# The last 14 units of two channel norms move from a tail into the row sweep behind them

## The reference: what is computed

```
x = x + conv0(_ln_c(x))              # norm 0, then four sweeps
t = tokens(x); t = t + ffn0(_ln_t(t))   # norm 1, mixture of experts
x = x + conv1(_ln_c(x))              # norm 2, then four sweeps
t = tokens(x); t = t + ffn1(_ln_t(t))   # norm 3, then a recurrence over 3600 tokens
```

## Time and profile before

| | |
|---|---|
| median of three runs | 4286.7 us (4286.59 to 4288.07) |
| profiled execution, its own time | 4284.66 us |
| its span (first to last instruction) | 4282.9 us |
| TensorE busy | 4142.7 us, 97% |
| VectorE busy | 1331.6 us, 31% |
| ScalarE busy | 2059.6 us, 48% |
| mean granted TensorE clock | 0.987 of full speed |
| loads of norm 0 into the ring | 144 with those of norm 1's source, 200 KB each, 3.7 us to landing |

### The profile page before, as it was taken

How to read it: one execution, slowest core, us unless ns; L and a number is a source line. 1 busy time by engine, 2 the same in 40 slices (tenths; PEclk the granted TensorE clock), 3 DMA queues, 4 the chain that set the end, 5 groups by cost and what they waited for, 6 DMA issues and landing times.

```text
span 4282.9 us, 138615 instructions
## 1 busy us (share of the span) xinstructions
PE 4142.7 (97%) x57258; PEld 3149.5 (74%) x57258; DVE 1331.6 (31%) x2528; ACT 2059.6 (48%) x8972; POOL 119.8 (3%) x243
## 2 busy tenths in 40 slices
PE   8999999998889999999998899999999999999999
PEld 2899999994452899999994366666666666666666
DVE  4555533334556655533335600000000000000000
ACT  5002344445545002334444366666666666666666
POOL 1000000000010000000000000000000000000000
PEclk9999999999999999999999899999999999999999
DMA  5000000003348000000006300000000000000000
GB/s 145 11 0 0 0 0 0 0 0 115 94 116 253 23 0 0 0 0 0 0 0 170 100 15 21 22 15 22 21 15 22 18 19 21 15 21 22 15 21 18
DMA packets 178458, 144.78 MB, mean 34 GB/s; under 512 B 110910, under 2 KB 177502, under 8 KB 178014
## 3 DMA queue, kind: packets, MB, share of 16 engines
q1 hardware_dynamic: 177486, 137.58, 12.2%
q10 hardware_dynamic: 528, 0.63, 0.1%
HBM read 79.19 MB, written 58.98 MB: 32 GB/s over the span
## 4 chain that ended last, share of the span: by engine, by line
PE 94%; DVE 3%; issue 1%; ACT 1%; DMA 0%; SPq 0%; POOL 0%; DVEq 0%; ACTq 0%; POOLq 0%
PE ps L945 23%; PE ps L795 21%; PE ps L773 18%; PE ps L864 16%; PE ps L859 3%; PE ps L577 2%; PE ps L569 1%; PE ps L744 1%; PE ps L588 1%; PE ps L598 1%; PE ps L612 1%; DVE rstd L1177 1%; PE ps L836 1%; PE ps L711 1%; PE ps L642 1%
## 5 line engine op out<-in xcount | busy, mean ns | idle before, releaser
L1157 ACT ACTIVATE xl<-ps 64x8 f32<-64x8 f32 x7200 | 1221.1, 171 | 613.0 <-PE ps L945 611.7
L945 PEld LDWEIGHTS ps<-xl,vt 65*32 65x32 f32 x28800 | 1042.9, 108 | 632.0 <-ACT xl L1157 392.7
L945 PE MATMUL ps<-xl,vt 65*32 65x8 f32 x28800 | 1448.8, 183 | 26.5
L864 PE MATMUL ps<-idle 128*32 128x256 bf16 (+1 forms) x5886 | 1370.0, 273 | 3.6 <-POOL ident L490 3.6
L795 PE MATMUL ps<-xl,taps 128*128 128x128 f32 (+2 forms) x7880 | 914.0, 279 | 4.7 <-DVE xl L1349 4.7
L795 PEld LDWEIGHTS ps<-xl,taps 128*128 128x128 f32 x7880 | 913.6, 191 | 5.4 <-issue 5.3
L773 PE MATMUL ps<-split 128*128 128x400 f32 x4140 | 780.9, 351 | 12.5 <-DVE split L1344 12.5
L773 PEld LDWEIGHTS ps<-split 128*128 128x128 f32 x4140 | 778.8, 190 | 16.2 <-issue 14.8
L1437 DVE TENSOR_TENSOR xl<-xl 64x320 f32<-64x320 f32 x180 | 125.1, 695 | 1710.0 <-ACT xl L1157 1710.0
L1012 ACT ACTIVATE img<-xl 128x144 f32 x788 | 365.7, 464 | 549.2 <-DVE xl L1326 549.2
L864 PEld LDWEIGHTS ps<-idle 128*32 128x32 bf16 x5886 | 583.3, 99 | 24.7 <-issue 10.9
(11 more groups left out here) (154 smaller groups left out, 1666.2 us busy)
## 6 DMA issues: line engine op xcount, KB each, us to landing
ring<-in_x_dram SPq DMA_DIRECT2D x144, 200.0 KB, 3.7
x_dram<-sums SPq DMA_DIRECT2D x144, 200.0 KB, 3.3
t_dram<-sums SPq DMA_DIRECT2D x72, 200.0 KB, 3.7
ring<-t_dram SPq DMA_DIRECT2D x72, 200.0 KB, 3.9
ring<-x_dram SPq DMA_DIRECT2D x72, 200.0 KB, 3.7
xl<-x_dram SPq DMA_DIRECT2D x45, 320.0 KB, 4.7
out_dram<-xl SPq DMA_DIRECT2D x45, 320.0 KB, 3.5
img<-in_L_ffn_weight_dram SPq DMA_DIRECT2D x4, 512.0 KB
```

The costliest lines, as they stand in the source:

```text
L864: pe.matmul(PS[bank][0:32, 0:n], idle[:, 0:32], idle[:, 0:n], start=True, stop=True)
L945: last = pe.matmul(PS[2 * s + h][c * 32:(c + 1) * 32, t * HB:(t + 1) * HB], vt[:, c * 32:(c + 1) * 32], prev, start=False, stop=True, skip ...
L1157: act.activation(yb[0:64, s, h * HB:(h + 1) * HB, t], PS[2 * s + h][0:64, t * HB:(t + 1) * HB], ACT.Sigmoid).then_inc(step_y[h], 1)
```

## The change

1. In norms 0 and 2 the loop ends with its 36th unit. The lag is 14 units, so 22 units are spread and scaled in the loop, and the last 14 inside the first 18 steps of the row sweep. After the second half of steps 0, 4, 6, 8, 10, 12 and 14, TensorE spreads one pair of units (four matmuls into banks 4 to 7); VectorE scales its four halves one by one, each behind the low part of a half of a step (`SCALE_AT`). These 18 steps are written out; the rest stay a loop.
2. A reciprocal is four instructions of 100 columns (`INVERSES`). Those of the last group in norms 0 and 2 also lie in the sweep, behind steps 2 to 4 (`INVERT_AT`). Variance groups have 10, 10, 10 and 6 units there (`GROUP`).
3. Units are taken in an order in which the first rows of all images are done first: norm 0 loads row chunk by row chunk (`group_of`), norm 2 spreads units 27 and 28 early (`ORDER`).
4. The 14 matmuls on zeros go, in norms 0, 2 and 3. The reduced taps, the line ends and the low taps are made inside the loop (at units 18, 20 and 22); the squares lie elsewhere in `xl` for it.
5. Norm 3 has a lag of 14 as well; norms 1 and 3 have the reciprocal in four parts (norm 3 two after one unit and two after the next). In the recurrence one wait for `added` stands ahead of a matmul instead of behind it.

```diff
-        LAG = NCH + 3
+        LAG = NCH + 5
+        INVERSES = 4
+        GROUP = {0: NCH + 1, 1: NCH, 2: NCH + 1, 3: NCH}
+        IN_NORM = UNITS - LAG
+        ROWS_SPREAD = (4, 5, 6, 7)
+        IN_ROWS = 18
+        PAIR_AT = {s: IN_NORM + 2 * j for j, s in enumerate((0, 4, 6, 8, 10, 12, 14))}
+        SCALE_AT = {(s + (h + j) // 2, (h + j) % 2): (p + j // 2, j % 2) for s, p in PAIR_AT.items() for h in (1,) for j in range(4)}
+        INVERT_AT = {(2, 1): 0, (3, 0): 1, (3, 1): 2, (4, 0): 3}
+        ORDER = {0: list(range(UNITS)),
+                 2: list(range(20)) + [27, 28] + [20, 21, 29, 30, 31] + list(range(22, 27)) + list(range(32, UNITS))}
...
         def group_of(i, n):
+            if i == 0:
+                return n % NG, n // NG
...
+        def spread_row(pe, i, p, h):
+            st, n = ln[i], ORDER[i][p]
+            if i == 0 and p == h == 0:
+                pe.wait_ge(spread_ready, 1)
+            pe.wait_ge(st.inverse, INVERSES * (place_of(i, n)[0] + 1))
+            if p == IN_NORM:
+                pe.wait_ge(st.normed, 2 * IN_NORM)
+            elif p:
+                pe.wait_ge(st.normed, 2 * p + h - (3 if p > IN_NORM + 1 else 1 if p < IN_NORM else h + 2))
+            spread_one(pe, i, n, h, row_spread_bank(p, h))
...
-                    if n == LAST:
-                        pe.wait_ge(st.kept, 2 * UNITS)
-                        for _ in range(14):
-                            keep_clock(pe, 512, SPARE)
...
-            for n in range(UNITS + LAG):
-                if n >= LAG:
+            for n in range(UNITS + 1):
+                if LAG <= n < UNITS:
                     spread_out(n - LAG)
...
+                    if k == 0 and isinstance(s, int) and s == 1:
+                        pe.wait_ge(ln[2 * l].std, NG)
                     pe.wait_ge(hi[l][h], s + LINES0[k])
...
                     products(0, 1).then_inc(conv[l][h], 1)
+                    if k == 0 and isinstance(s, int) and h == 1 and s in PAIR_AT:
+                        for j in range(4):
+                            spread_row(pe, 2 * l, PAIR_AT[s] + j // 2, j % 2)
...
+            if k == 0:
+                pe.wait_ge(ln[2 * l].kept, 2 * UNITS)
+            each_step(pe, k, step, IN_ROWS if k == 0 else 0)
...
+                            elif t == 2 * FILLS - 1:
+                                pe.wait_ge(added, seg + 2)
                             last = fill_input(pe, 1 - s, t)
                             if t == 2 * FILLS - 1:
                                 last.then_inc(filled, 1)
-                                pe.wait_ge(added, seg + 2)
...
-            dve.reciprocal(r0, r0).then_inc(ln[i].inverse, 1)
+            dve.reciprocal(rstd[:, a:a + n], rstd[:, a:a + n]).then_inc(ln[i].inverse, 1)
...
+                if n == LAG + 6:
+                    line_ends(dve, i // 2)
+                elif n == LAG + 8:
+                    low_taps(dve, i // 2)
+            first_line(dve, i // 2)
...
+                    if k == 0 and h == 0:
+                        if isinstance(s, int) and s < IN_ROWS:
+                            dve.wait_ge(ln[2 * l].normed, min(scaled_for(2 * l, s + 1), 2 * UNITS))
...
                     split_low(dve, l, h, line, s + (LINES0[k] + 1))
+                    if k == 0 and isinstance(s, int):
+                        if (s, h) in SCALE_AT:
+                            scale_row(dve, 2 * l, *SCALE_AT[s, h])
+                        if (s, h) in INVERT_AT:
+                            invert(dve, 2 * l, NG - 1, INVERT_AT[s, h])
```

More of the change, by code:

```diff
@@ L1211, in dve_token_norm @@
                         total(g * NCH + k)
-                    invert(dve, i, g)
+                    for part in range(INVERSES):
+                        invert(dve, i, g, part)
                     for k in range(NCH):
@@ L1226, in dve_token_norm, with scale_row, line_ends, low_taps @@
                     bn_take(dve, m, 1)
-                if 3 <= n < UNITS + 3 and n % NCH == 2:
-                    invert(dve, i, n // NCH - 1)
+                if NCH <= n < UNITS + NCH and 2 <= n % NCH < 4:
+                    for part in range(INVERSES // 2):
+                        invert(dve, i, n // NCH - 1, (n % NCH - 2) * INVERSES // 2 + part)
+        def scale_row(dve, i, p, h):
+            st, n = ln[i], ORDER[i][p]
+            dve.wait_ge(st.spread, 2 * p + h + 1)
+            dve.wait_ge(st.kept, 2 * n + h + 1)
+            rows = rows_of(i, n, h)
+            dve.tensor_tensor(rows, rows, pair(PS[row_spread_bank(p, h)][:, 0:CH]), ALU.mult).then_inc(st.normed, 1)
+        def line_ends(dve, l):
+            for h in range(2):
+                for part in range(2):
+                    for at in (0, EDGE + WP):
+                        dve.tensor_copy(split_line(h, part)[:, :, at:at + EDGE],
+                                        pick[:, 0:HB * EDGE].rearrange("p (b j) -> p b j", b=HB))
+        def low_taps(dve, l):
+            dve.wait_ge(taps_hi[l], 1)
+            dve.tensor_tensor(taps_part[1], taps[:, 0:2 * NO * 128], taps_part[0], ALU.subtract).then_inc(taps_lo[l], 1)
+        def first_line(dve, l):
+            dve.wait_ge(ln[2 * l].normed, scaled_for(2 * l, 0))
+            for h in range(2):
+                dve.sem_inc(state[l][h], 1)
+            for h in range(2):
+                line = row_at(l, h, 0)
+                dve.tensor_copy(line_pairs(h, 0), line).then_inc(hi[l][h], 1)
+                split_low(dve, l, h, line, 1)
         def dve_row_norm(dve, i):
@@ L1239, in total @@
                                       unit_of(ring, r)[:, v * CH:(v + 1) * CH], ALU.add).then_inc(st.summed, 1)
-            def scale(n):
-                for h in range(2):
-                    dve.wait_ge(st.spread, 2 * n + h + 1)
-                    rows = rows_of(i, n, h)
-                    dve.wait_ge(st.kept, 2 * n + h + 1)
-                    dve.tensor_tensor(rows, rows, pair(PS[spread_bank(n, h)][:, 0:CH]), ALU.mult).then_inc(st.normed, 1)
-            for n in range(UNITS + LAG):
-                if i == 2 and n < UNITS:
+            for n in range(UNITS):
+                if i == 2:
                     total(n)
                 if n >= LAG:
-                    scale(n - LAG)
-                if 3 <= n < UNITS + 3 and n % NCH == 2:
-                    invert(dve, i, n // NCH - 1)
+                    for h in range(2):
+                        scale_row(dve, i, n - LAG, h)
+                for since in (3, 4):
+                    g = place_of(i, n - since)[0]
+                    if n >= since and n - since + 1 == group_end(i, g):
+                        for part in range(INVERSES // 2):
+                            invert(dve, i, g, (since - 3) * INVERSES // 2 + part)
+                if n == LAG + 6:
[3 more added lines that the diff above has]
+            first_line(dve, i // 2)
         def dve_route(dve, g):
@@ L1315, in step @@
                     split_low(dve, l, h, line, s + (LINES0[k] + 1))
[L1317 removed]
+                    if k == 0 and isinstance(s, int):
[3 more added lines that the diff above has]
+                            invert(dve, 2 * l, NG - 1, INVERT_AT[s, h])
+            each_step(dve, k, step, IN_ROWS if k == 0 else 0)
         def dve_columns(dve, l, k):
```

90 lines of the change are left out of this document (39 added, 51 removed).

## The result

The changed kernel took **4235.7 us** (median of 4 runs, 4234.2 to 4242.5) against 4286.65 for the kernel before (4 runs beside it): a ratio of 0.9884 (95% interval 0.9867 to 0.9901), 50.9 us less. Forecast were 4249 and a range of 4237 to 4261: the direction is right, the time lies 1.3 us under the range, and the gain is 13.3 us larger than the sum of 37.6. The profiled execution is the longest of the four, 4242.5 (span 4240.8); the other three have spans of 4232.4 to 4234.7 and a mean clock of 0.989 to 0.990 instead of 0.987. So the two traces account for 42.1 us, and the medians differ by 8.8 more.

A forecast was written before the change was run, and what follows sets the result against it. TensorE, at 94% of the span, was taken as the bound. Tails and clock 48.1, spreads -14.0, loops +4.0, norm 3 -0.5 gave 37.6 us off 4286.7: 4249, with 8 in 10 between 4237 and 4261.

The forecast's parts named there:

- The recurrence has the same number of waits: Recurrence: the moved wait is for an addition issued ten steps earlier, so it changes nothing: 0.
- The tails: Ends of norms 0 and 2: the sweep follows the last variances without the serial tail, gaining 22.5 and 20.9 us.
- The slow clock at the sweep's head: Sweep's first half step takes 2.9 us instead of 5.54 and 4.99, gaining 2.6 and 2.1 us.
- The rival that the slow clock stays: Half clock falls again at or behind both sweeps' starts for as long as before: gain 19, 4267 us; chance 0.09.
- The spreads in the sweep: Row sweeps: 14 groups of four spreads, running side by side, cost TensorE 1.00 us each, 14.0 us lost.
- two by two: Row sweeps: the four spreads don't run side by side, so the 14 groups cost 26.2 us: 4261 us; chance 0.10.
- VectorE's part: Row sweeps: 28 scales at 0.55 us and four quarter reciprocals at 0.66 hide in 1.04 us of waiting: no cost.
- The loops: Loops of norms 0 and 2: 3.0 and 1.0 us, together 4.0 us gained, bounds 0 and 9.
- Later stalls on reciprocals: Norm 0's loop: stalls of 1.55 us and the like get shorter by halves; 0.2 us taken as gained.
- Norm 3: Norm 3: longer tail loses 4.0 us, loop gains 1.5, halved reciprocals 2.0: 0.5 us lost.
- Norm 1: Norm 1: the same columns inverted in four instructions, 0, at most 0.2 us for each of four groups.

The follow-up runs named there:

- e1: The kernel before, with only the recurrence's wait for `added` moved from step 8's first matmul to the last fill: 4270.7 us, ratio 0.9958.
- e2: The changed kernel with the recurrence's wait for `added` put back to where it was before: 4256.0 us, ratio 0.9918.
- e9: The changed kernel with the long fulfilled wait for `added` also on the second half's first matmul of steps 11 and 15 of each segment: 4268.9 us, ratio 0.9945.
- e4: The changed kernel with norm 3 alone back to a lag of 12 and its four quarter reciprocals in one unit: 4242.9 us, ratio 0.9887.
- e5: The changed kernel once more, unaltered, beside the kernel before: 4239.6 us, ratio 0.9881.
- e10: The changed kernel with low taps two units later and a lag of 16 in norms 0 and 2, norm 2's units reordered: 4223.9 us, ratio 0.9839.
- e7: The changed kernel with each of the sweep's groups of four spreads issued twice, the first four being work without use: 4243.6 us.
- e3: The changed kernel with the sweep's 14 groups of four spreads cut into 28 groups of two, behind successive half steps: 4251.1 us, ratio 0.9907.
- e8: The changed kernel with low taps two units later in norms 0 and 2, and a lag of 16 instead of 14 in norm 0: 4225.8 us, ratio 0.9848.
- e11: The changed kernel with norm 1's reciprocal in one instruction of 400 columns for each group instead of four of 100: 4235.0 us, ratio 0.9865.
- e6: The changed kernel with the low taps on VectorE two units later in norms 0 and 2: 4233.9 us, ratio 0.9867.

## Why the prediction missed, point by point

- **The step that failed: "The recurrence has the same number of waits; the moved one is for an addition that was issued when the segment began, ten steps earlier: 0."** It counted the waits and asked if they were fulfilled. What counts is the instruction that carries them: beside the wait for `step_y` the second one cost 0.08 us at that place, fulfilled or not (e1, e2, e9); on the fill it costs nothing that the steps show. The Trainium skill has the mechanism (Perfetto Trace Analysis, Identifying Dependency Chains: an instruction that waits for several engines may get EventSemaphore instructions ahead of it); the trace agrees, with 180 semaphore instructions there and 179 loads held up by "issue" in 180 segments. 0 was put where 14.7 stands, and no rival held it: with this term the same sum gives 4234, and the time lies well inside its range. (The last fill is in the step before the ninth, so "ten steps" was wrong too, without effect.)
- **The tails**, 22.5 and 20.9: measured 22.5 and 21.0 from the last square's end to the sweep. Right.
- **The slow clock at the sweep's head**, 2.6 and 2.1: 5.54 - 3.22 = 2.3 and 4.99 - 3.21 = 1.8. Right, 0.6 too large together, as the first half takes 3.2 and not 2.9. The rival that the slow clock stays is out in the profiled execution; in e4, e5, e9 and e10 block 0's sweep, and in e7 block 1's, still began at half clock, and the first half took 3.88 to 4.22 us: a small part of that rival's price.
- **The spreads in the sweep**, 14.0: 14 x 1.07 = 15.0. The sum of 1.00 a group was near, but by luck, for its parts were not: 0.67 for the passes instead of 0.87, and 0.40 for the mode both ways instead of 0.10 inside it and 0.13. That is why two spreads cost what four cost: side by side they share the passes, and the mode is paid by the group. The rival "two by two" would have cost 14 x 1.05 more (e3).
- **VectorE's part** was hidden, as said: half steps without spreads stay at 2.80 to 2.83, those with scales and reciprocals too.
- **The loops**, 4.0 gained: nothing that shows. The old loops took 91.47 and 111.76 us before, 87.40 and 114.74 in e1; the changed ones 89.50 and 113.91, 88.91 and 116.57 in e5. The step "Later stalls on reciprocals ... get shorter by halves" is wrong for norm 0: TensorE waited 4.7 us for reciprocals in norm 0 before (three times, at most 1.6) and 4.6 after. TensorE needs all four quarters, and VectorE has scales and, once, the low taps between them. More distance from the reciprocal ended these waits (e8), its pieces did not. In norm 2 the waits for reciprocals did fall, from 4.9 us to 0.8, but those for the summed units rose, from 3.9 (1.8 in e1) to 5.3, and the loop got no shorter.
- **Norm 3**, 0.5 lost: 0 to 0.4 in the executions without half clock at its start (167.78 in e3 and e8, 168.17 in e5), 3.0 in the one of the table, which has a clock of 0.64 over its first 9.5 us, and again 2.9 to 3.0 in e9, e10 and e11 with the same half clock. **Norm 1**, 0 to 0.8 lost: 1.8 in the table, the least of all; 1.8 to 4.2 in the ten later ones, e11 among them, against the 308.1 of the two kernels without. Its cause is open (e11).

The sum with measured terms: 43.5 + 4.1 - 15.0 + 0 - 0.4 + 14.7 = 46.9 us, less 1.8 for norm 1, is 45.1. With the 3.0 that norm 3 lost in the profiled execution, in place of 0.4, it is 42.5, and the trace gives 42.1. The medians give 50.9 and 50.5 (e5); those 5 to 6 us over 45.1 are of the size by which executions of one kernel differ (4237.0 to 4248.0 in e5). Between profiled executions the differences lie in half clock, late loads and the pace of the recurrence; those without a trace can't show it.

## What to carry to other kernels

On a serial chain of short steps, keep one wait to an instruction, and put any other on work beside the chain; idle time that the profile puts down to "issue", as often as a loop runs, is where to look. Work that changes the array's tiling pays a fixed price each time, so put as many such matmuls side by side as banks allow: the second pair was free. And where a loop stalls for a result that another engine makes in pieces, more distance between the two, with two units less to spread, bought 8 us in norm 0 where smaller pieces bought none.

## What the runs showed of the hardware that was not expected

- One moved wait was worth 14.7 us of 4287: 0.08 us in each of 180 places.
- The recurrence has two paces from one execution to the next: 0.505 us a step in the profiled executions of both kernels, e1, e3, e4 and e7 to e11, 0.507 in e2, e5 and e6, which makes some 6 us; the same code ran at either (1818.09 us in the changed kernel's first profile, 1824.08 in e5). What sets it is open.
- A wait of 2.20 us on TensorE was followed by 13.6 us at the lower clock, during which TensorE was busy throughout (13.60 of 13.60 us): what a short stall costs is more than its length. How much more differs from execution to execution: behind the same wait of 2.20 us in the same code, half clock lasted 13.7 us in e3, 10.3 in e2 and e11, and 3.4 in e4, e5, e7 and e9. In e1, with the old loop and its waits of up to 1.6 us for reciprocals, norm 0 has no such stretch behind them, while the kernel before has one of 13.7 us; so not each stall brings it.
